# Expert weights of a row on ScalarE, and the second token list's one-hots in contiguous columns, in an attention and mixture-of-experts kernel

## What is computed

```python
def _L0_xattn_ref(q, k, v):                       # q = layernorm(x), k = v = ctx
    score = jnp.einsum('bci,bcj->bij', k, q) / math.sqrt(l)
    score = jax.nn.softmax(score, axis=0)
    return jnp.einsum('bci,bij->bcj', v, score)
...
def _moe_forward(hidden_states, router_w, w1, b1, w2, b2):   # hidden = layernorm(x)
    logits = jnp.einsum('th,eh->te', x, router_w)
    topk_logits, topk_idx = jax.lax.top_k(logits, K)          # K = 2 of E = 8
    probs = jax.nn.softmax(topk_logits, axis=-1)
    combine = combine.at[jnp.arange(T)[:, None], topk_idx].add(probs.astype(x.dtype))
    hmid = jax.nn.gelu(jnp.einsum('th,efh->etf', x, w1) + b1[:, None, :], approximate=False)
    y = jnp.einsum('etf,ehf->eth', hmid, w2) + b2[:, None, :]
    out = jnp.einsum('eth,te->th', y, combine)
...
x = x + _L0_xattn_ref(_layernorm(x), ctx_1024, ctx_1024)
x = x + _L0_ffn_ref(_layernorm(x), router_w, w1, b1, w2, b2)
```

## Time and profile before

| | us |
|---|---|
| median of 3 runs | 800.47 (797.47 to 800.8) |
| profiled execution | 802.11 |
| its span, first to last instruction | 800.3 |
| busy PE / PEld | 715.2 (89%) / 610.8 (76%) |
| busy DVE / ACT / POOL | 611.1 (76%) / 404.7 (51%) / 539.4 (67%) |

### The profile page before, as it was taken

One profiled execution on the slowest core, in us unless ns is written; L12 is line 12 of the kernel. 1 busy time (PEld: TensorE's weight loads), 2 busy tenths in 40 slices (PEclk: granted clock), 3 DMA queues, 4 the chain that ended last, 5 costly groups with the idle time before them and its releaser, 6 DMA issues. The chain is left out here.

```text
span 800.3 us, 21890 instructions
## 1 busy us (share of the span) xinstructions
PE 715.2 (89%) x5691; PEld 610.8 (76%) x5692; DVE 611.1 (76%) x1482; ACT 404.7 (51%) x754; POOL 539.4 (67%) x665
## 2 busy tenths in 40 slices
PE   6997788699999955599999999999978999999995
PEld 4665555487777755399999999998957999999994
DVE  5998799889999978787777777727466677676764
ACT  3888677457666762154444444414433545444441
POOL 5775577778888840647777777754777777777763
PEclk9999899899999965599999999979999999999998
DMA  7884543148887750436555555542354444444440
GB/s 224 251 252 144 182 131 121 36 133 254 263 263 263 253 205 35 133 110 194 178 186 186 186 165 157 194 140 92 101 159 140 135 124 149 121 147 125 146 126 29
DMA packets 72927, 128.71 MB, mean 161 GB/s; under 512 B 9243, under 2 KB 46116, under 8 KB 72752
## 3 DMA queue, kind: packets, MB, share of 16 engines
q0 software_dynamic: 22528, 68.06, 27.9%
q1 hardware_dynamic: 50352, 60.07, 23.2%
HBM read 85.61 MB, written 47.24 MB: 166 GB/s over the span
## 5 line engine op out<-in xcount | busy, mean ns | idle before, releaser
L1054 ACT ACTIVATE work<-psum,b1T 128x256 f32<-128x256 f32 x304 | 127.8, 471 | 254.6 <-PE psum L682 254.6
L682 PE MATMUL psum<-work,w1T_high 128*128 128x256 f16 x1216 | 208.0, 276 | 2.5 <-ACT work L1062 2.5
L705 PE MATMUL psum<-w2T_high,slots 128*128 x1216 | 206.5, 275 | 0.8 <-issue 0.8
L682 PE MATMUL psum<-work,w1T_low 128*128 128x256 f16 x608 | 168.0, 276 | 0.0
L705 PE MATMUL psum<-w2T_low,slots 128*128 x608 | 167.2, 275 | 0.0
L682 PEld LDWEIGHTS psum<-work,w1T_high 128*128 x1216 | 120.3, 99 | 18.1 <-issue 3.0
L940 DVE CAST slots<-work 128x512 f16<-128x512 f32 x152 | 67.2, 442 | 84.3 <-ACT work L1054 81.8
L705 PEld LDWEIGHTS psum<-w2T_high,slots 128*128 128x128 f16 x1216 | 116.8, 99 | 14.4 <-issue 1.3
L531 POOL DMA_INDIRECT slots<-rows_first,slots x84 | 85.7, 1021 | 55.4 <-issue 52.3
L538 POOL DMA_INDIRECT rows_second<-slots x76 | 82.3, 1082 | 55.6 <-issue 31.3
L942 DVE TENSOR_TENSOR slots<-work,slots 128x512 f16<-128x512 f32 x152 | 106.5, 701 | 5.2
(11 more groups left out here) (126 smaller groups left out, 1179.5 us busy)
## 6 DMA issues: line engine op xcount, KB each, us to landing
rows_first<-slots SPq DMA_DIRECT2D x32, 520.0 KB, 3.0
work<-in_ctx SPq DMA_DIRECT2D x64, 256.0 KB, 3.3
slots<-in_x SPq DMA_DIRECT2D x32, 256.0 KB, 3.5
work<-in_x SPq DMA_DIRECT2D x32, 256.0 KB, 3.0
work<-in_L_ffn_w SPq DMA_DIRECT2D x32, 256.0 KB, 2.8
slots<-rows_first,slots POOLq DMA_INDIRECT x84, 3.6
rows_second<-slots POOLq DMA_INDIRECT x76
slots<-rows_second,slots POOLq DMA_INDIRECT x76, 3.5
```

Source lines behind the costliest of these rows:

```text
L682: mm = pe.matmul(h, w1T[pw][:, f, c, bass.ds(e * P, P)], xT[r2][:, (px * HC + c) * GROUP:(px * HC + c + 1) * GROUP], start=(c == 0 and px ...
L705: mm = pe.matmul(y, act16[r2][pa][:, f * GROUP + s * P:f * GROUP + (s + 1) * P], w2T[pw][:, f, bass.ds(e * DIM, DIM)], start=(f == 0 and p ...
L1054: last = act.activation(act32[r2][:, f * GROUP:(f + 1) * GROUP], psum[:, 2 + 2 * r2 + f // 2, (f % 2) * GROUP:(f % 2 + 1) * GROUP], ACT.Ge ...
```

## The change

Three things. The expert weights of a row are no longer made by one DVE product per pair of batches but by two ACT activations with `scale=inv`, between ACT's L1026 and L1031; ACT's pipeline runs one step longer. The one-hots of the second list are no longer written in four quarters in steps 0 to 3, but two batches at a time in steps 4 to 35, with the batch as the outermost index, so that a batch's 128 lanes and its 76 tiles are contiguous. And PE reads the second list's columns contiguously, and waits once for all of them. The first list is as it was.

```diff
+        LIST_FROM = LIST_STEP - BATCH // 2
...
                 for b in range(BATCH):
-                    q = b // w
-                    if b % w == 0:
-                        pe.wait_ge(r_lane, 4 * rnd + q + 1)
-                        pe.wait_ge(r_tiles, 4 * rnd + q + 1)
-                    mm = pe.matmul(psum[:, LIST_BANK[rnd], 0:TILES], lanes[:, :, b], tiles[:, :, b], start=(b == 0), stop=(b == BATCH - 1))
+                    if rnd:
+                        lane, tile = lane_hot[:, b * P:(b + 1) * P], tile_hot[:, b * TILES:(b + 1) * TILES]
+                        if b == 0:
+                            pe.wait_ge(r_lane, 4 + BATCH // 2)
+                            pe.wait_ge(r_tiles, 4 + BATCH // 2)
+                    else:
+                        lane, tile = lane_hot.rearrange("p (l b) -> p l b", b=BATCH)[:, :, b], tile_hot.rearrange("p (n b) -> p n b", b=BATCH)[:, :, b]
...
+                    mm = pe.matmul(psum[:, LIST_BANK[rnd], 0:TILES], lane, tile, start=(b == 0), stop=(b == BATCH - 1))
...
-                if live(i, k, L_P, PAIRS):
-                    m, r2 = i + k - L_P, (k - L_P) % 2
-                    dve.wait_ge(a_inv, m + 1)
-                    dve.tensor_tensor(slot2(m * 2, PR, EXPERTS), exps[:, r2, :, 0, :], inv[:, r2, :].unsqueeze(2).to_broadcast([P, 2, EXPERTS]),
-                                      ALU.mult).then_inc(a_comb, 1)
...
+            def one_hots_of_second(j):
+
+                b = BATCH + j * 2
+                one, two = tile_one[:, bass.ds(j * 2 * TILES, 2 * TILES)], tile_hot[:, bass.ds(j * 2 * TILES, 2 * TILES)]
+                as_tiles, as_lanes = "p (b n) -> p b n", "p (b l) -> p b l"
+                dve.tensor_tensor(one.rearrange(as_tiles, b=2), tile_of[:, bass.ds(b, 2)].unsqueeze(2).to_broadcast([P, 2, TILES]),
+                                  iota16[:, 0:TILES].unsqueeze(1).to_broadcast([P, 2, TILES]), ALU.is_equal).then_inc(r_ones, 1)
+                dve.tensor_tensor(lane_hot[:, bass.ds(j * 2 * P, 2 * P)].rearrange(as_lanes, b=2), lane_of[:, bass.ds(b, 2)].unsqueeze(2).to_broadcast([P, 2, P]),
+                                  iota16.unsqueeze(1).to_broadcast([P, 2, P]), ALU.is_equal).then_inc(r_lane, 1)
+                dve.wait_ge(r_ones, j + 5)
+                dve.tensor_tensor(two.rearrange(as_tiles, b=2), one.rearrange(as_tiles, b=2), mark[:, bass.ds(j * 2, 2)].unsqueeze(2).to_broadcast([P, 2, TILES]),
+                                  ALU.mult).then_inc(r_tiles, 1)
...
-                if isinstance(i, int) and i + k < 4:
-                    one_hots(1, i + k)
+                if rnd == 0 or (isinstance(i, int) and LIST_FROM <= i + k < LIST_STEP):
+                    one_hots_of_second(i + k - LIST_FROM)
...
+                if live(i, k, L_P, PAIRS):
+                    m, r2 = i + k - L_P, (k - L_P) % 2
+                    act.wait_ge(a_inv, m + 1)
+                    for j in range(2):
+                        last = act.activation(slot(m * 2 + j, PR, EXPERTS), exps[:, r2, j, 0, :], ACT.Identity, scale=inv[:, r2, j:j + 1])
+                    last.then_inc(a_comb, 1)
...
-            pipeline(act, PAIRS, RING, 2 * RING, L_LG, attend)
+            pipeline(act, PAIRS, RING, 2 * RING, L_P, attend)
```

More of the change, by code:

```diff
@@ L656, in list_tokens @@
             def list_tokens(rnd):
-                tiles = tile_hot.rearrange("p (n b) -> p n b", b=BATCH)
-                lanes = lane_hot.rearrange("p (l b) -> p l b", b=BATCH)
-                w = BATCH // 4
                 for b in range(BATCH):
-                    q = b // w
-                    if b % w == 0:
-                        pe.wait_ge(r_lane, 4 * rnd + q + 1)
-                        pe.wait_ge(r_tiles, 4 * rnd + q + 1)
-                    mm = pe.matmul(psum[:, LIST_BANK[rnd], 0:TILES], lanes[:, :, b], tiles[:, :, b], start=(b == 0), stop=(b == BATCH - 1))
+                    if rnd:
[5 more added lines that the diff above has]
+                        lane, tile = lane_hot.rearrange("p (l b) -> p l b", b=BATCH)[:, :, b], tile_hot.rearrange("p (n b) -> p n b", b=BATCH)[:, :, b]
+                        if b % 16 == 0:
+                            pe.wait_ge(r_lane, b // 16 + 1)
+                            pe.wait_ge(r_tiles, b // 16 + 1)
+                    mm = pe.matmul(psum[:, LIST_BANK[rnd], 0:TILES], lane, tile, start=(b == 0), stop=(b == BATCH - 1))
                 mm.then_inc(r_list, 1)
```

## The result

The changed kernel takes **787.48 us** (median of 4 runs, 786.93 to 790.57), the kernel before in the same comparison 800.63 (797.47 to 802.15, 4 runs). The ratio is 0.985, with a 95% interval of 0.982 to 0.988: some 10 to 14 us faster. The prediction was 789, with 784 to 796 as its range.

What follows compares the result with a forecast made beforehand. The attention stage was taken as paced by a GpSimd-VectorE ring, the expert stage by TensorE. 2.0 + 0 + 0 + 0 + 7.0 + 2.5 = 11.5 us off the median 800.47 gave 789 us, range 784 to 796.

Steps and rivals of the forecast that it cites:

- Part 1: Attention stage, expert weights to ScalarE: GpSimd holds L818 instead of L813 and idles 0.34 us, not 0.42; 2.0 us gained.
- the ring: Attention stage's pace: GpSimd's product L493, VectorE's L823, GpSimd's normalisation, then L493 again.
- The tail: End of the attention stage, GpSimd's L506 after the stores: moves with the rest, 0 us, -1.5 to +1.5.
- Part 2: Start of the expert stage: second list's one-hots leave steps 0 to 3, where their work was covered; 0 us gained.
- Part 3: Steps 4 to 35: one-hots return in 32 pieces, 0.98 us a step on VectorE, hidden by TensorE; 0 us.
- Part 4: Second list's 64 matmuls on TensorE read contiguous columns: 10.64 us becomes 3.6, 7.0 us gained.
- The clock: 24 matmuls behind the second list: a shorter list ends before TensorE's clock falls; 2.5 us gained, 0 if it falls.
- (c): Attention stage: L818 isn't held and the ring is cut, 8.8 us gained instead of 2.0; about 782, chance 0.06.
- (d): Second list gets only a little shorter, or the clock falls anyway; about 795, chance 0.08.
- (e): Second list: the old columns weren't the matter, nothing of Part 4 comes; 798, chance 0.06.
- (a): Expert stage, round one: VectorE or GpSimd sets the pace, costing 3 to 6 us; about 794, chance 0.13.
- (b): End of each of 32 expert steps: VectorE becomes the bound outright, kernel slower; about 804, chance 0.05.

Runs made afterwards that it cites:

- part 1 alone: The kernel before with only the expert weights moved to ScalarE, the lists as before: 798.18 us, ratio 0.998.
- parts 2 to 4 alone: The changed kernel with the expert weights' product (L813) back on VectorE: 787.95 us, ratio 0.985.

## Why the prediction was right, step by step

**Part 1, 2.0 us: right in size and mechanism.** The cast takes over the hold, GpSimd's idle time goes from 0.42 to 0.34 us, the stage is 2.07 us shorter, and 2.05 with part 1 alone. ScalarE's pair takes 0.40 us, a little over its bound of 0.36, and is covered while the ring sets the pace.

**The tail, 0: mis-sized, and one step of its argument was wrong.** It cost 0.55 us, within its bounds, in the changed kernel and with part 1 alone. The prediction had the stores of finished rows wait for weights that are "now ready sooner". They are ready later. GpSimd's L506, now L507, waits until the rows of the first 28 pairs are stored. The last of these weights, VectorE's before and ScalarE's after:

```profile
285.34 0.16 DVE L813 TENSOR_TENSOR slots<-smax 128x16 f32<-128x16 f32 x1
```

```profile
283.91 0.48 ACT L1043 ACTIVATE slots<-smax 128x8 f32<-128x8 f32 x2
```

They end at 285.50 and 284.39, which is 4.62 and 5.08 us after the cast that opens the tail, and GpSimd starts 3.01 us behind them in both kernels (at 288.51 and 287.40). With part 1 alone it is 3.01 again, and 3.02 with the product back on VectorE. So 0.46 of the 0.55 us is ScalarE's pair, in a step in which nothing covers it.

**Part 2, 0: right.** 187.67 and 187.66 us up to the list. TensorE's idle stretch there still ends with ScalarE (1.22 us before, 1.58 after, 1.20 with parts 2 to 4 alone). VectorE has 9.59 us to spare ahead of its first split, which gains nobody anything:

```profile
333.88 0.43 DVE L952 CAST slots<-work 128x512 f16<-128x512 f32 x1 [9.59 <-ACT work L1072]
```

**Part 3, 0: right, with a piece sized too large.** 0.79 us instead of 0.98: consecutive instructions overlap, so that the 0.13 us fixed in each don't add up. GpSimd wasn't slowed: 29.84 us busy in 40 before, 29.40 after. The prediction's picture, in which a gather under one-hots gets longer by a part, did not hold for such pieces in a row, where one took 17.96 us; nothing in it foresaw this, and that pieces laid between the groups never met it (none over 1.32 us from 345 us to the second list) is luck.

**Part 4, the list, 7.0 us: right in mechanism, mis-sized.** 8.09. The term that was off is the 56 ns of a matmul, taken from transposes with 128 moving columns; with 76 it is 38 to 40 ns, near the lower bound given, 2.0 us for the list. The 81 ns for a stream of pairs at 128 columns in the Trainium skill, TensorE: Matmul & The Clock Gate, section Back-to-back issue gap, is twice what this stream of 76 columns took. The prediction's remark that no row with contiguous operands is that slow overlooked its own L705, at 109 ns each.

**The clock, 2.5 us: right in this trace, in part by luck.** 5.10 to 2.62 us is 2.48. But behind the same strided list the product took 4.43 us with part 1 alone and 4.19 with `bn_aggr` moved up in the kernel before, so the term is 1.6 to 2.5 us. And the argument was that a short list is over before the point at which the clock fell, 5.5 us in. With the lanes alone strided the clock fell some 2.0 us into the list, with both arrays strided in pieces some 0.7 us, behind an idle time of 1.25 and 1.78 us. The contiguous list of 2.5 us kept the full clock even where TensorE had idled for 1.12 us ahead of it, in the kernel with two more products a step. So it isn't shown that the shortness is what kept it.

**The sum, 11.5 us: right,** and 11.5 in the two profiled executions; by the medians it is 13.2. The list gave 1.1 more, the tail took 0.55, and this execution started 0.50 later. That they cancel to the tenth is luck. **The rivals:** (c) fell with the cast's 0.88 us, (d) and (e) with the list's 2.55 us at full clock; (a) and (b) weren't met, but two more products of 256 columns in a step make them true.

**The change of rounds** carried the gain on, as foretold, but isn't constant. From the last transposes of round one to those from which round two runs without a wait it takes 34.10 us before, 34.26 after, 32.54 with part 1 alone, 31.72 with parts 2 to 4, 33.31 and 31.87 with `bn_aggr` first. TensorE waits for rows there; after:

```profile
574.21 1.04 PE L697 MATMUL psum<-ident,slots 128*128 128x128 f16 x8 [4.10 <-DMA slots<-rows_second,slots]
```

Over all fourteen traces it is 31.65 to 35.98. No edit touches this stretch, and why it differs stays open. A term of half a us is told by landmarks ahead of this place, not by whole times.

## What to carry to other kernels

Before taking an instruction off a full engine, look at the one behind it: if the same neighbour can hold that one too, the hold moves and only the rest is gained. What TensorE reads should be contiguous in both operands; where that makes its producer slower, cut the producer's work into pieces and lay them where another engine sets the pace, with the room there counted first. A term taken from a single trace is one draw: the 5.10 us behind the strided list were 4.19 in another.

## What the hardware showed that was not expected

- In a stream, a matmul of 128 lanes and 76 f16 columns takes 38 to 40 ns from contiguous operands, 89 with only the weights, 131 with only the moving columns and 166 with both at a step of 64 elements. The strided ones don't slow down when the granted clock falls from 1.00 to 0.50 (16 records in 2 us, then 18).
- VectorE's one-hot of 256 f16 columns takes 0.42 us written contiguously and 1.30 written at a step of 64 elements.
- An indirect gather was held for 17.96 us under the last 63 of 72 VectorE instructions of 0.30 to 0.42 us without a gap between them (the one ahead of it took 1.04), and gathers took 1.07 under the same work in instructions with twice the columns.
